# One pass of 32 chunks over both directions of a state-space scan

## The chip, the cores and the metric

The kernel runs on one core of a Trainium2 chip (trn2). The metric is the time of one execution on the device in microseconds, the median of several runs.

## What is computed

A block of three parts over 4 sequences of 2048 tokens with 256 channels: a feed-forward half (attention with 16 heads, then a mixture of 8 experts), a bidirectional state-space layer, and the feed-forward half again. The change touches the state-space layer alone, whose reference, cut to what matters, is:

```python
def _mamba_branch(xz, conv_w, conv_b, x_proj_w, dt_w, dt_b, A_log, D):
    x, z = jnp.split(xz, 2, axis=1)
    x = _silu(causal depthwise conv of 4 taps(x, conv_w) + conv_b)
    dt, Bm, Cm = split(einsum('bdl,ed->bel', x, x_proj_w))      # 16 + 16 + 16 rows
    dt = softplus(einsum('brl,dr->bdl', dt, dt_w) + dt_b)
    A = -jnp.exp(A_log)
    def step(h, inp):
        dt_t, B_t, C_t, u_t = inp
        h = jnp.exp(dt_t[..., None] * A) * h + (dt_t * u_t)[..., None] * B_t[:, None, :]
        return (h, jnp.einsum('bdn,bn->bd', h, C_t))
    ...
    y = ys + D[None, :, None] * x
    return y * _silu(z)
h = _layernorm(x, norm_w, norm_b)
xz = jnp.einsum('bld,ed->bel', h, in_proj_w)
y_f = _mamba_branch(xz, ...the forward weights)
y_r = _mamba_branch(xz[..., ::-1], ...the reverse weights)[..., ::-1]
out = jnp.einsum('bdl,od->blo', y_f + y_r, out_proj_w)
return x + out
```

There are 512 inner channels (4 groups of 128, m = 0 to 3) and 16 states (n = 0 to 15).

## The kernel before

The program is a row of phases. Each phase has its own tiles and semaphores and ends in a barrier of all engines. `mamba_in` writes the inputs of the scans to DRAM (`xp`, padded by three columns, and `zs`, the silu of z). Then `mamba_scan` is called twice, as phase `scan_f` with the forward weights, which writes `y`, and as phase `scan_r` with the reverse weights, which reads `y` and `zs` and writes `yz`, the sum of both directions times silu(z). `mamba_out` multiplies by the output weights.

One call works through N = 16 chunks of 512 tokens, four to a sequence. The five engines each run their own list of the same chunks; nothing but semaphores ties them together, and each engine issues in the order of its list. `in_steps` (L1511) makes that list: the four chunks of the first sequence are written out one after another, the other twelve run in a hardware loop (`Fori`) of three passes with four chunks in the body. In the reverse direction `place` (L1507) counts the chunks from the end.

A chunk is 16 steps, one a state. In step n:

- ACT makes the decays, exp(dt A), into two PSUM banks in turn (L1831), four a step.
- DVE multiplies dt u with the row of b for the next state (`times_b`, L1889; POOL does it for the states in `POOL_N`) and runs the scan along the tokens (L1923), four a step, into one of four buffers `h`. The direction is in the order in which the columns are read (`flip`).
- POOL multiplies h with the row of c (L1628). The rows come from SP, which loads them broadcast (`row_c`, `row_b`) from a small DRAM tensor.
- PE adds h up over the states in PSUM banks 0 to 3 (`sum_state`, L1707), against an identity.

Between these, every engine prepares the chunks to come: PE does the convolution of chunk i + 2 (`conv`, L1647, in halves in steps 7 to 14, through one bank that ACT empties in `conv_out`, L1753, in steps 9, 11, 13 and 15), the projection of chunk i + 1 (`x_proj`, L1664, step 0; `dt_proj`, L1674, steps 3 to 6) and the row of b (`row_b`, L1682). ACT adds the silu (L1757) and the softplus. The window of x for chunk i + 2 is loaded at step 0, the preparation of a chunk past the last one wraps round to chunk 0 and is thrown away.

In step 1 `skip` (L1697) opens the sums with D u, after y of the chunk before has been read. In the reverse direction it also adds the other direction's y (`yi`, L1701). The finished sum is read by ACT in the forward direction (`read_y`, L1797) and by DVE in the reverse one, times silu(z) (L1896), and SP stores it in step 3 (L1536). In the reverse direction SP loads zs into the store's buffer `yo` (L1577) and the next y into `yi` (L1579) in step 5.

Ahead of the first chunk stands a preparation of its own: the weights are loaded (L1550 to L1554), DVE builds the diagonal matrices for the convolution (L1866) and for D (L1870) and negates exp(A_log) (L1873), and chunks 0 and 1 are convolved, chunk 0 also projected, before the first scan.

## Time and profile before

| | us |
|---|---|
| median of 3 runs | 8743.57 |
| lowest and highest of them | 8741.03, 8743.65 |
| the profiled execution | 8750.53 |
| its span in the trace | 8748.8 |
| first scan of the forward direction | 2702.82 |
| first scan of the reverse direction | 4469.96 |
| last result of the reverse direction sent off | 6201.55 |

The profile is of one execution. The chip's engines are PE (TensorE), DVE (VectorE), ACT (ScalarE), POOL (GpSimd) and SP (SyncE, which issues loads and stores here). A row names the line of the kernel, the engine, the operation, output <- inputs and shapes.
### The profile page before, as it was taken

What the parts mean: (1) busy time and instruction counts of PE and PEld (TensorE: products, weight loads), DVE (VectorE), ACT (ScalarE), POOL (GpSimd) and SP (SyncE); (2) the same over time, 40 slices, a digit from 0 to 9 for tenths busy, and PEclk for the clock granted to TensorE, in tenths of its full rate; (3) what the DMA queues carried; (4) which work ended last, traced back from release to release, by engine and by line L of the source; (5) the groups of instructions that cost most, each with busy time, mean ns of one, the idle gap of its engine ahead of it and who ended that gap; (6) DMA issues with size and microseconds to landing.
All of it is one profiled execution on the core that took longest, in us unless ns stands there. A gap on an engine that the chain in (4) does not pass through costs nothing. (4 is left out here: it accounts for less than half of the span.)

```text
span 8748.8 us, 137191 instructions
## 1 busy us (share of the span) xinstructions
PE 7384.9 (84%) x39098; PEld 2876.4 (33%) x39098; DVE 7557.3 (86%) x11017; ACT 5055.9 (58%) x7663; POOL 3676.0 (42%) x1812
## 2 busy tenths in 40 slices
PE   6788888889997888888878888888777888888799
PEld 3222222225543333333323333333542222222255
DVE  6898888878867999999979999999358988888888
ACT  3577777762235666666655555555224777777622
POOL 0010011100006999999969999999300100110000
PEclk8799999999999999999999999999987999999999
DMA  6001001012262222222223333333561011011122
GB/s 171 17 19 20 19 19 26 19 42 77 72 210 88 83 83 82 82 83 84 83 92 100 102 103 100 100 102 100 171 189 17 19 20 19 19 21 23 42 67 67
DMA packets 554170, 623.35 MB, mean 71 GB/s; under 512 B 205376, under 2 KB 363328, under 8 KB 549408
## 3 DMA queue, kind: packets, MB, share of 16 engines
q1 hardware_dynamic: 548896, 581.63, 22.8%
q0 software_dynamic: 4608, 33.56, 1.9%
q8 instruction: 330, 5.41, 0.3%
q14 instruction: 336, 2.75, 0.1%
HBM read 416.65 MB, written 163.76 MB: 66 GB/s over the span
## 5 line engine op out<-in xcount | busy, mean ns | idle before, releaser
L833 DVE TENSOR_REDUCE ffn_att_mx<-psum 128x1 f32<-128x512 f32 (+2 forms) x4840 | 2915.6, 655 | 389.7 <-PE psum L666 197.4
L794 ACT ACTIVATE ffn_att_e<-psum,unscale 128x1024 f32<-128x1024 f32 (+3 forms) x2560 | 2384.0, 983 | 843.9 <-PE psum L739 842.9
L632 POOL TENSOR_SCALAR_AFFINE_SELECT ffn_att_e<-ffn_att_e 128x512 f32<-128x512 f32 x512 | 324.6, 634 | 3125.8 <-ACT ffn_att_e L794 3125.8
L666 PE MATMUL psum<-ffn_att_k,ffn_att_q 48*128 48x512 f16 (+3 forms) x5384 | 989.1, 368 | 611.2 <-DVE ffn_att_mx L833 545.2
L1628 POOL TENSOR_TENSOR scan_r_h<-scan_r_h,scan_r_cs 128x1024 f32<-128x1024 f32 x512 | 1207.1, 2447 | 148.0 <-ACT scan_r_state L1791 144.7
L705 PE MATMUL psum<-ffn_att_e,ffn_att_v 128*32 128x512 f32 (+3 forms) x10240 | 1248.5, 558 | 10.0 <-issue 3.8
L1628 POOL TENSOR_TENSOR scan_f_h<-scan_f_h,scan_f_cs 128x1024 f32<-128x1024 f32 x512 | 1204.4, 2444 | 118.8 <-ACT scan_f_state L1791 116.1
L1707 PE MATMUL psum<-scan_f_h,ident 128*128 128x512 f32 x2048 | 989.0, 623 | 84.0 <-POOL scan_f_h L1628 83.1
L1707 PE MATMUL psum<-scan_r_h,ident 128*128 128x512 f32 x2048 | 975.0, 617 | 78.1 <-POOL scan_r_h L1628 77.5
L1831 ACT ACTIVATE psum<-scan_r_dt,scan_r_an 128x512 f32<-128x512 f32 x1024 | 698.1, 682 | 456.2 <-DVE scan_r_h L1923 456.0
L1831 ACT ACTIVATE psum<-scan_f_dt,scan_f_an 128x512 f32<-128x512 f32 x1024 | 697.6, 681 | 423.8 <-DVE scan_f_h L1923 423.3
L666 PEld LDWEIGHTS psum<-ffn_att_k,ffn_att_q 48*128 48x128 f16 x5384 | 263.9, 94 | 2002.3 <-DVE ffn_att_mx L833 1884.7
L1923 DVE TENSOR_TENSOR_SCAN scan_r_h<-psum,scan_r_state,scan_r_db 128x512 f32<-128x512 f32 x704 | 844.5, 1261 | 5.5 <-ACT psum L1831 5.5
L1923 DVE TENSOR_TENSOR_SCAN scan_f_h<-psum,scan_f_state,scan_f_db 128x512 f32<-128x512 f32 x704 | 840.5, 1261 | 9.0 <-ACT psum L1831 9.0
L739 PE MATMUL psum<-ffn_att_q,ffn_att_k 50*128 50x512 f16 (+3 forms) x5120 | 728.1, 355 | 32.9 <-issue 29.5
L1707 PEld LDWEIGHTS psum<-scan_f_h,ident 128*128 128x128 f32 x2048 | 384.7, 197 | 670.2 <-issue 434.1
L1707 PEld LDWEIGHTS psum<-scan_r_h,ident 128*128 128x128 f32 x2048 | 383.9, 195 | 648.8 <-issue 439.2
L1180 DVE SCALAR_TENSOR_TENSOR ffn_out_acc<-psum,ffn_out_comb,ffn_out_acc 128x256 f32<-128x256 f32 x896 | 433.4, 484 | 65.2 <-PE psum L1045 29.6
L1889 DVE TENSOR_TENSOR scan_r_db<-scan_r_du,psum 128x2048 f32<-128x2048 f32 x177 | 404.9, 2288 | 25.1 <-PE psum L1682 4.8
L1889 DVE TENSOR_TENSOR scan_f_db<-scan_f_du,psum 128x2048 f32<-128x2048 f32 x177 | 404.9, 2288 | 24.7 <-DVE scan_f_h L1923 3.9
L1923 DVE TENSOR_TENSOR_SCAN scan_f_h<-psum,scan_f_state,scan_f_dbp 128x512 f32<-128x512 f32 x320 | 385.9, 1264 | 30.8 <-ACT psum L1831 30.8
L1923 DVE TENSOR_TENSOR_SCAN scan_r_h<-psum,scan_r_state,scan_r_dbp 128x512 f32<-128x512 f32 x320 | 385.9, 1264 | 30.8 <-ACT psum L1831 30.8
(240 smaller groups left out, 9216.5 us busy)
## 6 DMA issues: line engine op xcount, KB each, us to landing
scan_f_cs<-scan_f_bcd SPq DMA_DIRECT2D x264, 256.0 KB, 3.2
scan_r_cs<-scan_r_bcd SPq DMA_DIRECT2D x264, 256.0 KB, 3.3
scan_f_bs<-scan_f_bcd SPq DMA_DIRECT2D x82, 256.0 KB, 3.5
scan_r_bs<-scan_r_bcd SPq DMA_DIRECT2D x82, 256.0 KB, 3.5
scan_f_win<-xp SPq DMA_DIRECT2D x18, 1036.0 KB, 6.6
scan_r_win<-xp SPq DMA_DIRECT2D x18, 1036.0 KB, 7.0
ffn_att_q<-q_parts SPq DMA_DIRECT2D x144, 128.0 KB, 2.9
mamba_out_ys<-yz SPq DMA_DIRECT2D x18, 1024.0 KB, 7.3
```

The source lines that it names most:

```text
L632: nc.gpsimd.affine_select(out=part, in_=part, compare_op=ALU.is_ge, fill=0.0, base=0, pattern=[[0, REP], [1, P]], channel_multiplier=-1).t ...
L666: ins = nc.tensor.matmul(psum[:, turns[hh], j * w:(j + 1) * w], q[at, i // HALF, pair, i % HALF * P:(i % HALF + 1) * P], k[at, c * P:c * P ...
L705: ins = nc.tensor.matmul(psum[32 * h:32 * h + VW, BANK_O, off:CH], V[par][:, kb, :], E[:, s % PB, h, off:CH], start=kb == 0, stop=closes(s ...
L739: ins = nc.tensor.matmul(psum[:, h, off:CH], k[at, kb * P:(kb + 1) * P], q[at, qb * CH // (HALF * P), h // 2, qb * CH % (HALF * P) + off:q ...
L794: nc.scalar.activation(E[:, s % PB, 2 * hp:2 * hp + 2, off:CH], psum[:, 2 * hp:2 * hp + 2, off:CH], ACT.Exp, scale=unscale[:, 0:1]).then_i ...
L833: nc.vector.reduce_max(mx[:, hh * 2 + pairs[0]:hh * 2 + pairs[1], i // HALF, i % HALF, c // TT], psum[:, turn, 0:(pairs[1] - pairs[0]) * w ...
L1180: nc.vector.scalar_tensor_tensor(acc[:, e % 2, :], psum[:, BANKS_E[(n // 2) % 4], (e % 2) * C:(e % 2 + 1) * C], comb[par][:, t, e:e + 1], ...
L1628: nc.gpsimd.tensor_tensor(hh, hh, cs[:, n % NCS, :].unsqueeze(1).to_broadcast([P, 2, CH]), ALU.mult).then_inc(hc_ready, 1)
L1707: ins = nc.tensor.matmul(psum[:, m, :], ident[:, :], h[n % NH][:, m, :], start=False, stop=n == DS - 1)
L1831: nc.scalar.activation(psum[:, BANK_A + k % 2, :], dt[par][:, m, :], ACT.Exp, scale=an[:, m, n:n + 1]).then_inc(decay, 1)
L1889: nc.vector.tensor_tensor(db[b_turn(par, n)][:, :, :], du[par][:, :, :], psum[:, BANK_B, :].unsqueeze(1).to_broadcast([P, DM, CH]), ALU.mu ...
L1923: nc.vector.tensor_tensor_scan(h[n % NH][:, m, flip], psum[:, BANK_A + k % 2, flip], made_b[:, m, flip], state[:, n, m:m + 1], ALU.mult, A ...
```

## The change

The two calls become one, `mamba_scans`, a single phase over M = 32 chunks: 0 to 15 forward, 16 to 31 reverse. Each step gets a function `way(k)`, which says whether the chunk k ahead of the current one is a reverse one; every use of weights, window offset, read order and position asks it. So in forward chunks 14 and 15 the preparation of chunks 16 and 17 uses the reverse weights. The list of chunks is now: four written out, a loop of two passes (4 to 11), eight written out (12 to 19), a loop of three passes (20 to 31).

Both directions' weights, diagonals and negated A are made ahead of chunk 0, those of the reverse direction behind the others'. The addition of the other direction's y becomes a part of its own, `add_other`, in step 9 instead of step 1, and the load of the next `yi` moves from step 5 to step 11. The first `yi` and `zs` are loaded in step 5 of chunk 16.

```diff
-def mamba_scan(nc, tag, psum, ident, reverse, xp, zs, y_other, y_out, conv_w, conv_b, xprojT, dtT, dt_b, a_log, d_w, B, S):
+def mamba_scans(nc, tag, psum, ident, xp, zs, y, yz, weights, B, S):
     N = B * NC
+    M = 2 * N
-    LAST = 0 if reverse else CH - 1
-    flip = slice(None, None, -1) if reverse else slice(None)
+    LAST = (CH - 1, 0)
+    FLIP = (slice(None), slice(None, None, -1))
-    PE_X, PE_DT, PE_CONV = 0, 3, 7
+    PE_X, PE_DT, PE_CONV, PE_Y, SP_Y = 0, 3, 7, 9, 11
...
         def in_steps(eng, step):
-            for r in range(NC):
-                step(r, r % 2, r == 0, r == 0, r == NC - 1)
-            if B > 1:
-                with eng.Fori(0, B - 1) as b:
-                    for r in range(NC):
-                        step(b * NC + NC + r, r % 2, False, r == 0, r == NC - 1)
+            def alone(i):
+                step(i, i % 2, i == 0, i % NC == 0, i % NC == NC - 1, lambda k: i + k >= N)
+
+            def batches(first, count, rev):
+                if count > 0:
+                    with eng.Fori(0, count) as b:
+                        for r in range(NC):
+                            step(b * NC + first + r, r % 2, False, r == 0, r == NC - 1, lambda k: rev)
+            for i in range(NC):
+                alone(i)
+            batches(NC, B - 2, False)
+            for i in range(max(N - NC, NC), N + NC):
+                alone(i)
+            batches(N + NC, B - 1, True)
...
-                if reverse:
-                    sp.dma_start(yi[:, :, :], cols(y_other, place(0))).then_inc(y_in, 16)
+                sp.dma_start(cw[1][:, :, :], weights[1][0]).then_inc(w_in[1], 16)
...
-                        if n == 5 and reverse:
-                            if not first:
-                                hold(sp, stored, 16 * i, sp_passed)
-                            sp.dma_start(yo[:, :, :], cols(zs, place(i))).then_inc(z_in, 16)
-                            hold(sp, y_added, DM * (i + 1), sp_passed)
-                            sp.dma_start(yi[:, :, :], cols(y_other, place(i + 1))).then_inc(y_in, 16)
+                        if n == 5 and way(0):
+                            hold(sp, stored, 16 * i, sp_passed)
+                            sp.dma_start(yo[:, :, :], cols(zs, place(i, True))).then_inc(z_in, 16)
+                            if not way(-1):
+                                sp.dma_start(yi[:, :, :], cols(y, place(i, True))).then_inc(y_in, 16)
+                        if n == SP_Y and way(0):
+                            hold(sp, y_added, DM * (i - N + 1), sp_passed)
+                            sp.dma_start(yi[:, :, :], cols(y, place(i + 1, True))).then_inc(y_in, 16)
...
-                    if reverse:
-                        pe.wait_ge(y_in, 16 * (i + 1))
-                        for m in range(DM):
-                            nc.tensor.matmul(psum[:, m, :], ident[:, :], yi[:, m, :], start=False, stop=False).then_inc(y_added, 1)
+                def add_other(i):
+                    pe.wait_ge(y_in, 16 * (i - N + 1))
+                    for m in range(DM):
+                        nc.tensor.matmul(psum[:, m, :], ident[:, :], yi[:, m, :], start=False, stop=False).then_inc(y_added, 1)
...
                         if n == 1:
-                            skip(i, par, first)
+                            skip(i, par, first, way(0))
+                        if n == PE_Y and way(0):
+                            add_other(i)
...
                 first_silu(1, FREE)
-                act.wait_ge(a_neg, 1)
+                act.wait_ge(w_in[1], 112)
+                nc.scalar.activation(an[1][:, :, :], an[1][:, :, :], ACT.Exp).then_inc(a_exp, 1)
+                act.wait_ge(a_neg, 2)
...
-                        if not reverse and n == 1 and not first:
+                        if n == 1 and not first and not way(-1):
                             read_y(i - 1, m)
...
+                dve.wait_ge(w_in[1], 112)
+                diagonals(1)
+                skips(1)
                 dve.wait_ge(cleared, 2)
...
                 times_b(0, 0, 0)
+                negate(1)
...
-                        if reverse and n == 1 and not first:
+                        if n == 1 and not first and way(-1):
                             read_y(i - 1, m)
```

On ACT, at the change of direction. Before, between the last decay of the forward scan (`scan_f_an`) and the first of the reverse one (L1831 with `scan_r_an`), stand a loop's end, the last reads of y, and the second phase's preparation:

```order
L1831 ACTIVATE psum<-scan_f_dt,scan_f_an 128x512
L1518 REGISTER_ALU
L1518 COMPARE_AND_BRANCH
L1791 ACTIVATE scan_f_state<-scan_f_zeros 128x2
L1797 ACTIVATE scan_f_yo<-psum 128x512 x4
L1526 UNCONDITIONAL_BRANCH
L1745 UNCONDITIONAL_BRANCH
L1747 ACT_TABLE_LOAD
L1749 ACTIVATE scan_r_an<-scan_r_al 128x64
L1801 ACT_TABLE_LOAD
L1801 ACTIVATE scan_r_u<-psum,scan_r_cb 128x512 x4
L1802 ACT_TABLE_LOAD
```

Now, at the same place (`scan_anf` is the forward A, `scan_anr` and `scan_cbr` the reverse A and convolution bias):

```order
L1771 ACTIVATE scan_u<-psum,scan_cbr 128x512
L1775 ACT_TABLE_LOAD
L1775 ACTIVATE scan_u<-scan_u 128x2048
L1776 ACT_TABLE_LOAD
L1851 ACTIVATE psum<-scan_dt,scan_anf 128x512
L1809 ACTIVATE scan_state<-scan_zeros 128x2
L1851 ACTIVATE psum<-scan_dt,scan_anf 128x512
L1851 ACTIVATE psum<-scan_dt,scan_anr 128x512
L1809 ACTIVATE scan_state<-scan_zeros 128x2
L1851 ACTIVATE psum<-scan_dt,scan_anr 128x512 x2
```

The first reverse decay directly follows the last forward one; the reads of y have gone into step 1 of the next chunk.

On DVE, ahead of the first chunk of all. Before:

```order
L1866 TENSOR_SCALAR scan_f_cwd<-ident,scan_f_cw 128x128 x16
L1870 TENSOR_SCALAR scan_f_dwd<-ident,scan_f_dw 128x128 x4
L1873 TENSOR_SCALAR scan_f_an<-scan_f_an 128x64
L1879 TENSOR_TENSOR psum<-psum,scan_f_bc 32x512
L1883 TENSOR_TENSOR scan_f_bc<-psum,scan_f_mid 32x512
L1900 TENSOR_TENSOR scan_f_dt<-scan_f_sp,scan_f_dt 128x2048
L1902 TENSOR_TENSOR scan_f_du<-scan_f_dt,scan_f_u 128x2048
L1889 TENSOR_TENSOR scan_f_db<-scan_f_du,psum 128x2048 x2
L1923 SCALAR_TENSOR_TENSOR scan_f_h<-psum,scan_f_state,scan_f_db 128x512 x4
```

Now (the last letter of `cwd`, `dwd` and `an` is the direction):

```order
L1888 TENSOR_SCALAR scan_dwdf<-ident,scan_dwf 128x128 x4
L1893 TENSOR_SCALAR scan_anf<-scan_anf 128x64
L1883 TENSOR_SCALAR scan_cwdr<-ident,scan_cwr 128x128 x16
L1888 TENSOR_SCALAR scan_dwdr<-ident,scan_dwr 128x128 x4
L1907 TENSOR_TENSOR psum<-psum,scan_bc 32x512
L1911 TENSOR_TENSOR scan_bc<-psum,scan_mid 32x512
L1928 TENSOR_TENSOR scan_dt<-scan_sp,scan_dt 128x2048
L1930 TENSOR_TENSOR scan_du<-scan_dt,scan_u 128x2048
L1917 TENSOR_TENSOR scan_db<-scan_du,psum 128x2048
L1893 TENSOR_SCALAR scan_anr<-scan_anr 128x64
L1917 TENSOR_TENSOR scan_db<-scan_du,psum 128x2048
L1953 SCALAR_TENSOR_TENSOR scan_h<-psum,scan_state,scan_db 128x512 x4
```

Twenty diagonals have come in ahead of the split of b, and a negation between the two products with b.

On PE, steps 8 to 10 of a reverse chunk. Before:

```order
L1647 MATMUL psum<-scan_r_win,scan_r_cwd 128x512 x2
L1707 MATMUL psum<-scan_r_h,ident 128x512 x4
L1682 MATMUL psum<-scan_r_bc,scan_r_sel 128x512
L1647 MATMUL psum<-scan_r_win,scan_r_cwd 128x512 x2
L1707 MATMUL psum<-scan_r_h,ident 128x512 x4
L1682 MATMUL psum<-scan_r_bc,scan_r_sel 128x512
L1647 MATMUL psum<-scan_r_win,scan_r_cwd 128x512 x2
```

Now:

```order
L1657 MATMUL psum<-scan_win,scan_cwdr 128x512 x2
L1719 MATMUL psum<-scan_h,ident 128x512 x4
L1692 MATMUL psum<-scan_bc,scan_sel 128x512
L1657 MATMUL psum<-scan_win,scan_cwdr 128x512 x2
L1713 MATMUL psum<-scan_yi,ident 128x512 x4
L1719 MATMUL psum<-scan_h,ident 128x512 x4
L1692 MATMUL psum<-scan_bc,scan_sel 128x512
L1657 MATMUL psum<-scan_win,scan_cwdr 128x512 x2
```

The four matmuls on `yi`, which stood in step 1 behind those on `dwd`, stand between the half convolution and the sums of step 9.

## Rows read from the trace of the kernel before

**Rows 1.** The page's first part: busy us (share of the span) x instructions.

```profile
PE 7384.9 (84%) x39098; PEld 2876.4 (33%) x39098; DVE 7557.3 (86%) x11017; ACT 5055.9 (58%) x7663; POOL 3676.0 (42%) x1812
```

**Rows 2.** Stretches between first scans: us from:to, length, busy us.

```profile
core 0: us, PE busy (x) PEld busy (x) DVE busy (x) ACT busy (x) POOL busy (x), PEclk, DMA share, GB/s
2702.82:2807.68 104.86, 87.72 (x187) 33.70 (x186) 102.07 (x78) 64.73 (x124) 99.21 (x38) 0.95 0.21 63
2807.68:2912.53 104.85, 89.47 (x197) 33.86 (x195) 102.06 (x79) 66.07 (x127) 102.11 (x40) 0.98 0.28 84
3227.97:3333.62 105.65, 92.21 (x195) 35.03 (x195) 102.06 (x78) 66.06 (x127) 101.97 (x41) 0.95 0.29 83
3439.28:3546.54 107.26, 91.68 (x196) 35.27 (x195) 102.05 (x78) 66.03 (x127) 103.28 (x41) 0.95 0.28 83
3972.22:4291.70 319.48, 269.25 (x585) 102.24 (x585) 306.40 (x232) 198.07 (x381) 304.60 (x118) 0.98 0.28 82
4291.70:4469.96 178.26, 136.92 (x286) 52.69 (x286) 120.40 (x108) 91.54 (x165) 110.31 (x44) 0.90 0.31 95
...
5438.63:5546.67 108.04, 92.33 (x203) 35.52 (x203) 104.45 (x83) 64.39 (x123) 102.21 (x41) 0.98 0.33 101
```

**Rows 3.** Order of time at the change of direction, DVE: start, us, engine.

```profile
4392.90 2.46 DVE L1923 TENSOR_TENSOR_SCAN scan_f_h<-psum,scan_f_state,scan_f_dbp 128x512 f32<-128x512 f32 x2 [1.89 <-ACT psum L1831]
...
4408.42 0.91 DVE L1860 MEMSET scan_r_sel<- 96x1024 uint32 x1 [13.05 <-PEq L51]
...
4469.96 4.81 DVE L1923 TENSOR_TENSOR_SCAN scan_r_h<-psum,scan_r_state,scan_r_db 128x512 f32<-128x512 f32 x4 [0.29 <-ACT psum L1831]
```

**Rows 4.** Order of time at the start of the forward phase.

```profile
2643.69 8.28 DVE L1866 TENSOR_SCALAR scan_f_cwd<-ident,scan_f_cw 128x128 f32<-128x128 f32 x16 [0.30 <-DMA scan_f_cw<-in_m_conv_w_f]
...
2649.17 0.26 ACT L1749 ACTIVATE scan_f_an<-scan_f_al 128x64 f32<-128x64 f32 x1 [5.77 <-DMA scan_f_wt<-in_m_dtT_f]
...
2652.68 0.19 DVE L1873 TENSOR_SCALAR scan_f_an<-scan_f_an 128x64 f32<-128x64 f32 x1
...
2674.51 0.69 DVE L1879 TENSOR_TENSOR psum<-psum,scan_f_bc 32x512 f32<-32x512 f32 x1 [21.64 <-ACT scan_f_bc L1764]
...
2700.24 2.29 DVE L1889 TENSOR_TENSOR scan_f_db<-scan_f_du,psum 128x2048 f32<-128x2048 f32 x1 [3.30 <-PE psum L1682]
2700.73 1.28 ACT L1802 ACT_TABLE_LOAD   x1
```

**Rows 5.** Order of time without a loop's turn, at one, at the exit.

```profile
3439.74 3.63 PE L1664 MATMUL psum<-scan_f_u,scan_f_wx 128*48 128x512 f32 x8
...
3544.34 2.29 DVE L1889 TENSOR_TENSOR scan_f_db<-scan_f_du,psum 128x2048 f32<-128x2048 f32 x1 [1.39 <-issue]
...
3547.68 5.26 PE L1664 MATMUL psum<-scan_f_u,scan_f_wx 128*48 128x512 f32 x8
...
6193.69 7.03 PE L1707 MATMUL psum<-scan_r_h,ident 128*128 128x512 f32 x16
```

**Rows 6.** Order of time, a reverse chunk: PE, then one of ACT.

```profile
5453.96 3.60 PE L1701 MATMUL psum<-scan_r_yi,ident 128*128 128x512 f32 x8
...
5506.81 0.39 PE L1682 MATMUL psum<-scan_r_bc,scan_r_sel 96*128 96x512 bf16 x1 [1.59 <-DVE scan_r_db L1889]
5507.04 1.88 PE L1647 MATMUL psum<-scan_r_win,scan_r_cwd 128*128 128x512 f32 x4
...
5513.01 1.98 PE L1647 MATMUL psum<-scan_r_win,scan_r_cwd 128*128 128x512 f32 x4 [0.66 <-ACT scan_r_u L1753]
...
5525.77 0.39 PE L1682 MATMUL psum<-scan_r_bc,scan_r_sel 96*128 96x512 bf16 x1 [1.31 <-DVE scan_r_db L1889]
...
5512.29 0.67 ACT L1753 ACTIVATE scan_r_u<-psum,scan_r_cb 128x512 f32<-128x512 f32 x1
```

**Rows 7.** The loads into yi: issues, and time to landing.

```profile
L1579 SPq DMA_DIRECT2D scan_r_yi<-y x16: 388/394/1965, 4507.7 to 6128.5; - x16
...
DMA to landing us min/median/max: 6.3/9.5/10.9
```

195 lines of the change are left out of this document (101 added, 94 removed).

## The prediction

> **What bounds the kernel now.** I read the page first, for the busy shares [rows 1]: VectorE (DVE) is busy 86% of the span and TensorE (PE) 84%, but that mean covers attention, projection and scan stages with different limits, so it prices nothing here. The change touches the two scans alone, so the second view is a table of stretches cut at the first DVE scan instruction of a chunk [rows 2]. A chunk (512 tokens, 16 states) of the forward scan takes 104.86 us where its code stands straight in the program and 105.65 us in the hardware loop; DVE is busy 102.07 and 102.06 us of that, PE 87.72 and 92.21, ACT 64.73 and 66.06. DVE is the bound, with 2.8 and 3.6 us of idle per chunk. POOL is nearly as busy (99 to 102 us of a chunk), but it works on states that DVE has already scanned. The reverse chunk takes 108.04 us, since DVE also reads y out there (104.45 us busy), and its idle is 3.6 us again.
>
> Third, the order of time at the change of direction [rows 3]. The last forward scan pair starts at 4392.90 and takes 2.46, so DVE's stream ends at 4395.36. DVE then does nothing for 13.05 us (rest of PE and POOL work, the store of y, the barrier of the phase) until the memset of the reverse phase at 4408.42, and its first scan runs at 4469.96. 74.60 us pass between two scans that in the middle of a direction follow each other directly. In that stretch no engine is a bound for long: it is a chain through all of them, load, diagonals, convolution, silu, projection, softplus, b.
>
> **The change part by part.**
>
> *The boundary.* What the reverse phase computes in those 74.60 us for its first chunk is what every chunk computes for the next one. The forward scan's last chunk already does it today: its steps load, convolve and project a chunk that nobody scans (the position wraps round). So preparing reverse chunk 0 there adds no instruction to the last forward chunk; it only makes the work useful, with other weights. The stretch from the first scan of forward chunk 15 to the first scan of the reverse direction, now 178.26 us [rows 2], becomes one ordinary chunk. The nearest row is a chunk of straight code, since chunks 12 to 19 are written out now: 104.86. Gain 178.26 - 104.86 = 73.40. The reads of y of the last forward chunk stay on ACT and lie in step 1 of the next chunk, as in the other forward chunks, where they cost DVE nothing (104.86 for chunk 0, which has none of them, and 104.85 for chunk 1, which has). The new loads of that chunk: zs into yo and y into yi are issued in step 5, 37.7 us after the first scan (4507.7 for a chunk that starts at 4469.96 [rows 7]), and y into yi lands at most 10.9 us later, at 48.6; PE wants it in step 9, about 63 us after the first scan (for a chunk that starts at 5438.63: PE's row at 5506.81 less its idle of 1.59 and the sums of one state, 3.6 as for four matmuls, is 5501.6 [rows 6]). The store of y that they follow is issued in step 3. 14 us of cover; 0.
>
> *Forward chunks 12 to 15 leave the loop.* Chunks 12 to 14 take 319.48 us together [rows 2]; three straight ones take 3 x 104.86 = 314.58. Gain 4.90. Part of it is a loop turn's echo: after a turn PE comes late, its projection takes 5.26 us against 3.63 [rows 5], the last sums of y stand behind it, and ACT's read of them holds up the next decay.
>
> *One turn of the forward loop becomes an exit.* A chunk that ends in a turn takes 107.26 us against 105.65 [rows 2], and in it DVE shows 1.39 us of "issue" before the first instruction of the next pass [rows 5]. Chunk 11 now ends in a branch not taken. The only exit that the trace shows on a busy engine is PE's out of the reverse loop: 16 records without a gap across it, from 6193.69 for 7.03 us [rows 5]. I take 0 for it, so a gain of 107.26 - 105.65 = 1.61; the bound from the other side is the turn itself and its echo in chunk 12, which is what chunks 12 to 14 take over three loop chunks, 319.48 - 3 x 105.65 = 2.53: so up to 4.1 us less gain. A page of the Trainium skill bears on this (Runtime: NRT & Kernel Launch, Instruction fetch mechanics): fetch ahead is sequential and hidden, and a taken branch whose target is not held costs a fetch. By it the exit and the extra straight code are free, as I have them; were an exit priced as a turn, the gain would be those 4.1 us smaller. The trace agrees on the turn (1.39 us) and on straight code (104.86 against 105.65).
>
> *The set-up of two directions at the start.* Added: seven weight loads on SP, 16 + 4 diagonals and one negation on DVE, one Exp on ACT. SP: the loads stand behind the first direction's, and SP has nothing to do until the second window load, which waits for the first convolutions. DVE: the weights of today had landed by 2649.17, 5.5 us after the first of them [rows 4]; as much again for the seven more is 2654.7. Sixteen diagonals take 8.28 us [rows 4], twenty 10.4, so they end by 2665.1, and DVE's next work is at 2674.51, after 21.64 us of idle. Cover 9.4 us: 0, and if it were gone, 10.4. PE starts on diagonals of the first direction alone and is not held. Not covered is the tail: ACT's Exp of the reverse A comes after the table load that ends at 2702.01 (2700.73 + 1.28), takes 0.26, and DVE must negate the result (0.19 us) ahead of its second product with b, because the negation stands ahead of it in DVE's order. That product started at 2700.24; it now starts at 2702.01 + 0.26 + 0.19 and a tenth for a semaphore, some 2702.5, and its 2.29 us put the first scan at about 2704.8 instead of 2702.82. PE and SP shift with it. Cost 2.0.
>
> *The other direction's y is added in step 9, not step 1.* PE only: four matmuls, 3.60 us [rows 6], in 16 reverse chunks. At step 1 they cost DVE nothing today (the chunk's idle is 3.6 in both directions), so nothing is gained there. At step 9 they fall between half a convolution and the sums. PE then lags 3.60 us, less the 1.59 us that it waited for DVE before the next row of b at 5506.81: 2.0. The half convolution behind it would end at 5508.92 + 2.0 = 5510.9, and ACT fetches its result at 5512.29 [rows 6]: 1.4 us of cover. With the idle of 0.66 and 1.31 us that follow, PE is level again at 5526. DVE needs the sums of state 8 at state 12 (four h buffers), some 10 us later. 0, at most 3.6 a chunk. SP's load of the next yi moves to step 11, behind a wait for that addition; behind this wait stand rows of c fetched eight states ahead, and the yi itself is wanted a chunk later. 0.
>
> Sum: -73.40 - 4.90 - 1.61 + 2.0 = -77.9 us. The profiled execution took 8750.5 (span 8748.8) and should become 8672.6 (span 8670.9); it lies 7 us above the median of the runs, 8743.57, from which I take the same 77.9: **8665.7 us**.
>
> **The rivals.**
>
> 1. *The exit costs like a turn*, with its echo: 4.1 us less, 8669.8. For it: nobody has seen DVE or ACT leave a loop busy. Against: PE's exit.
> 2. *The second set-up is not hidden*: the small loads come late or the diagonals are in front of something: +10.4, 8676. For it: many small loads behind a 1 MB window. Against: 9.4 us of cover. The Trainium skill (DMA: Bandwidth & Descriptors, Specifications) has transfers under 512 B below line rate; by it the seven loads (conv_b's rows are 16 B) would land later than their bytes suggest, which the first seven's 5.5 us already contain.
> 3. *The boundary is only half closed*: the first reverse chunk waits at some hand-over that the forward chunks don't have (zs or y into the buffers, stored before read). With half of 73.4 lost, 8702. Against: 14 us of cover.
> 4. *The addition in step 9 comes through once a chunk*: 16 x 3.6 = 58 us given back, 8723, at the edge of what can be told from no change. Against: 1.4 us of cover at ACT, and 2.0 of lag in all, so it needs a worse lag than the rows show, for instance a PE as slow just there as in the projection at 3547.68.
> 5. *It comes through three times a chunk, and the kernel is slower.* PE never makes up the lag, and each of ACT's three fetches of a convolution in steps 11, 13 and 15 waits the full 3.6 us; ACT issues in order, so the decays and with them DVE wait. 16 x 10.8 = 173 us, 8839. The change is a loss from 78/16 = 4.9 us a chunk on. For it: PE is busy 92 us of 108. Against: 15.7 us of PE idle a chunk, 3.6 of them in the three gaps of [rows 6].
>
> **How the numbers follow.** Forecast 0.68; exit 0.10; set-up 0.09; half closed 0.04; once a chunk 0.06; three times 0.03. The range takes the forecast and rivals 1 and 2 (0.87 together). Its low end is the forecast less what the remaining forward turn may cost less (1.6, and a late chunk behind it, 2.5) and 4 us for the scatter of runs; its high end is rival 2 with the same: 8658 to 8680. About 0.2%, 17.5 us, is what a measurement can tell from no change. Faster by more: forecast, rivals 1 to 3 and half of 4, 0.94; within: the other half of 4, 0.03; slower: 0.03.
>
> **What would show it.** In the trace after: the first scan near 2704.8, and no idle of DVE over 3 us between two scans until the end of the reverse direction; 104.9 us from the first scan of chunk 15 to the first of chunk 16; chunks 12 to 14 at 104.9 each; reverse chunks in the loop at 108.0 as before; no memsets and no phase barrier between the directions. Wrong if reverse chunks are longer than 108.0 with ACT's convolution fetch showing idle behind PE, or if chunk 16 shows PE waiting for yi.

## The result, and the profile after

The changed kernel takes 8701.18 us (median of 5 runs, 8692.50 to 8705.29) against 8743.65 (5 runs beside it, 8741.03 to 8765.72): ratio 0.9942, interval 0.9928 to 0.9957. It is faster by 42 us; the forecast had 78. The profiled execution took 8692.50, its span is 8690.8.

The page's first part, as [rows 1] of before:

```profile
span 8690.8 us, 135894 instructions
...
PE 7349.9 (85%) x39016; PEld 2870.6 (33%) x39016; DVE 7538.8 (87%) x11009; ACT 5034.7 (58%) x7630; POOL 3672.6 (42%) x1809
```

DVE's busy time fell by 18.5 us and PE's by 35.0; the span fell by 58.0. So idle time went too. The two traced executions lie apart by more than the medians do (58.0 against 42.5 us): the one of before is 7 us above its median, the one of after the fastest of its five. Where did the time go? The first thing to do is to cut both traces at the first work of each phase:

| from / to | before | after | difference |
|---|---|---|---|
| start / first work of the scan phase | 2642.11 | 2641.77 | -0.3 |
| scan phase / first of `mamba_out` | 3565.21 | 3489.34 | -75.9 |
| `mamba_out` | 171.85 | 171.62 | -0.2 |
| second feed-forward, preparation | 153.02 | 153.32 | +0.3 |
| second attention (`ffn_att`) | 1746.78 | 1726.89 | -19.9 |
| second `ffn_out` to the end | 469.85 | 507.86 | +38.0 |
| sum | | | -58.0 |

The scan phase gave what was forecast for it, within 2 us. Two later phases, whose code nobody touched, differ by twenty and by forty microseconds with opposite signs.

*The scans.* Stretches between first scans, after, in the columns of [rows 2]: chunk 11 (now an exit), chunks 12 to 14, chunk 15, a reverse chunk in the loop, and one whose predecessor ended in a turn; last the second `ffn_out`:

```profile
core 0: us, PE busy (x) PEld busy (x) DVE busy (x) ACT busy (x) POOL busy (x), PEclk, DMA share, GB/s
...
3865.20:3970.75 105.55, 90.98 (x195) 34.63 (x195) 102.05 (x78) 66.05 (x127) 101.89 (x41) 0.97 0.28 83
3970.75:4286.51 315.76, 274.04 (x585) 105.65 (x585) 306.18 (x232) 198.00 (x381) 305.65 (x118) 0.95 0.28 83
4286.51:4391.35 104.84, 90.62 (x196) 34.49 (x195) 102.05 (x78) 66.03 (x127) 101.97 (x40) 0.97 0.28 84
5361.30:5469.33 108.03, 93.90 (x204) 36.40 (x203) 104.44 (x82) 64.41 (x123) 102.20 (x41) 0.97 0.32 101
5251.46:5361.30 109.84, 95.71 (x203) 36.93 (x203) 104.56 (x83) 64.36 (x123) 100.96 (x40) 0.94 0.33 99
8182.94:8687.10 504.16, 462.31 (x2304) 262.45 (x2304) 382.41 (x964) 128.87 (x256) 35.30 (x18) 0.95 0.23 71
```

Chunk 15, which was 178.26 us to the first reverse scan, is an ordinary chunk: 104.84. Order of time there, the last forward scan and the first reverse one (compare [rows 3]):

```profile
4386.65 2.46 DVE L1953 TENSOR_TENSOR_SCAN scan_h<-psum,scan_state,scan_dbp 128x512 f32<-128x512 f32 x2 [2.05 <-ACT psum L1851]
...
4387.97 0.69 ACT L1851 ACTIVATE psum<-scan_dt,scan_anr 128x512 f32<-128x512 f32 x1 [0.65 <-DVE scan_h L1953]
...
4389.15 2.29 DVE L1917 TENSOR_TENSOR scan_db<-scan_du,psum 128x2048 f32<-128x2048 f32 x1
...
4391.35 4.80 DVE L1953 TENSOR_TENSOR_SCAN scan_h<-psum,scan_state,scan_db 128x512 f32<-128x512 f32 x4
```

DVE idles 2.05 us before the last forward pair (1.89 before), and from there its instructions follow each other; ACT makes the first reverse decay (`scan_anr`) during that pair. The 13.05 us of the hand-over and everything to 4469.96 are gone.

The start of the phase, DVE and ACT (compare [rows 4]):

```profile
2674.06 0.69 DVE L1907 TENSOR_TENSOR psum<-psum,scan_bc 32x512 f32<-32x512 f32 x1 [17.62 <-ACT scan_bc L1782]
...
2700.23 1.28 ACT L1820 ACT_TABLE_LOAD   x1
2701.53 0.26 ACT L1834 ACTIVATE scan_anr<-scan_anr 128x64 f32<-128x64 f32 x1
2701.81 0.20 DVE L1893 TENSOR_SCALAR scan_anr<-scan_anr 128x64 f32<-128x64 f32 x1 [5.33 <-ACT scan_anr L1834]
2701.92 2.28 DVE L1917 TENSOR_TENSOR scan_db<-scan_du,psum 128x2048 f32<-128x2048 f32 x1
...
2704.12 3.63 DVE L1953 TENSOR_TENSOR_SCAN scan_h<-psum,scan_state,scan_db 128x512 f32<-128x512 f32 x3
```

The twenty extra diagonals are hidden: DVE is still idle for 17.62 us before the split of b at 2674.06. The tail is seen as priced: table load, Exp (`scan_anr`), negation, product, one after the other, the first scan at 2704.12. That is 62.35 us after the phase's first work against 60.71.

Step 9 of the same reverse chunk as in [rows 6] (PE, then ACT's fetch of the convolution):

```profile
5424.71 3.60 PE L1713 MATMUL psum<-scan_yi,ident 128*128 128x512 f32 x8
...
5428.15 3.60 PE L1719 MATMUL psum<-scan_h,ident 128*128 128x512 f32 x8
...
5431.58 0.38 PE L1692 MATMUL psum<-scan_bc,scan_sel 96*128 96x512 bf16 x1
...
5431.80 1.88 PE L1657 MATMUL psum<-scan_win,scan_cwdr 128*128 128x512 f32 x4
...
5434.96 0.67 ACT L1771 ACTIVATE scan_u<-psum,scan_cbr 128x512 f32<-128x512 f32 x1
```

The addition of `yi` stands between half a convolution and the sums; the half convolution behind it ends at 5433.68, ACT fetches it at 5434.96. 1.3 us of cover are left and DVE's chunk is 108.03.

*The second `ffn_out`.* DVE's waits in it, and the order of time around one of them on DVE and on PE:

```profile
engine line waited for: us in total, times, longest us
DVE ffn_out_acc L1180 <- issue: 42.3, 6, 7.5
...
8271.03 0.19 DVE L1168 TENSOR_TENSOR ffn_out_comb<-ffn_out_lg,ffn_out_rden 128x32 f32<-128x32 f32 x1 [0.23 <-DVE ffn_out_lg L1165]
8278.47 0.48 DVE L1180 SCALAR_TENSOR_TENSOR ffn_out_acc<-psum,ffn_out_comb,ffn_out_h 128x256 f32<-128x256 f32 x1 [7.25 <-issue]
...
8279.54 0.61 PE L1045 MATMUL psum<-ffn_out_eh,ffn_out_uh 128*128 128x512 f16 x1 [3.96 <-DVE ffn_out_acc L1180]
```

Before the first of the accumulations of an expert (L1180) DVE stands still for 7.25 us though it waits for no semaphore; its inputs are there, and PE's next matmul (L1045) waits 3.96 us for DVE. The place is the turn of the loop: the trace's record of DVE's own branches has the branch back to the loop's start at 8271.13 and the next instruction at 8278.16. This happens six times, at each of the six turns of the seven passes, 61 us apart (8278.5, 8339.7, 8400.8, 8463.0, 8524.2, 8585.7), 42.3 us in all. Before, the same stretch had none of it, nor has the first `ffn_out` of the changed kernel (466.44 us), which runs the same code. Both `ffn_out` of before, DVE busy as long as after:

```profile
1916.64:2383.16 466.52, 450.00 (x2304) 260.78 (x2304) 382.69 (x964) 128.88 (x256) 35.23 (x18) 0.98 0.24 76
8278.97:8745.20 466.23, 450.02 (x2304) 260.80 (x2304) 382.67 (x964) 128.86 (x256) 35.25 (x18) 0.97 0.24 76
```

The trace also shows what arrives in such a wait. The page's list of DMA queues has two of the kind `instruction`; this is one of them before, after, and in the first experiment below:

```profile
q14 instruction: 336, 2.75, 0.1%
...
q14 instruction: 359, 2.94, 0.1%
...
q14 instruction: 330, 2.70, 0.1%
```

In the changed kernel it moves 8192 bytes five times after each of the six turns of the second `ffn_out`: after the first turn at 3.09, 5.01, 7.64, 10.43 and 38.65 us from the branch, with DVE going on at 7.03. In the kernel before there is not one transfer of that kind between the first and the last turn of either `ffn_out`.

*The second attention.* The stretch of before, then that of after:

```profile
6532.19:8276.41 1744.22, 1415.73 (x12821) 415.39 (x12821) 1515.10 (x2626) 1228.58 (x1378) 163.32 (x258) 0.93 0.11 20
```

```profile
6456.05:8180.37 1724.32, 1397.29 (x12821) 411.12 (x12821) 1512.68 (x2626) 1229.57 (x1378) 164.06 (x258) 0.94 0.12 20
```

19.9 us shorter with as many instructions; DVE is busy 2.4 us less, PE 18.4 us less, ACT 1.0 us more. PE's busy time points at its clock: the trace's record of the granted clock has 237.5 us of this stretch at the lower of the two levels (1.2 GHz) before and 190.3 us after.

### The profile page after: what moved, and what is told of

Its sections match the earlier page's. It is cut to its first block and busy times, and to the rows that moved or that the text cites. A ratio compares the mean times of both kernels' runs of the same rounds, so it can differ in the third digit from the quotient of the medians.

```text
span 8690.8 us, 135894 instructions
## 1 busy us (share of the span) xinstructions
PE 7349.9 (85%) x39016; PEld 2870.6 (33%) x39016; DVE 7538.8 (87%) x11009; ACT 5034.7 (58%) x7630; POOL 3672.6 (42%) x1809
## 5 line engine op out<-in xcount | busy, mean ns | idle before, releaser
L1638 POOL TENSOR_TENSOR scan_h<-scan_h,scan_cs 128x1024 f32<-128x1024 f32 x1024 | 2412.6, 2449 | 206.0 <-ACT scan_state L1809 200.6
L1719 PE MATMUL psum<-scan_h,ident 128*128 128x512 f32 x4096 | 1985.8, 626 | 158.1 <-POOL scan_h L1638 156.9
L1953 DVE TENSOR_TENSOR_SCAN scan_h<-psum,scan_state,scan_db 128x512 f32<-128x512 f32 x1408 | 1684.6, 1260 | 10.5 <-ACT psum L1851 10.5
L1719 PEld LDWEIGHTS psum<-scan_h,ident 128*128 128x128 f32 x4096 | 781.8, 199 | 1325.1 <-issue 906.0
L1851 ACT ACTIVATE psum<-scan_dt,scan_anr 128x512 f32<-128x512 f32 x1024 | 698.0, 682 | 456.1 <-DVE scan_h L1953 455.6
L1851 ACT ACTIVATE psum<-scan_dt,scan_anf 128x512 f32<-128x512 f32 x1024 | 697.5, 681 | 421.4 <-DVE scan_h L1953 420.9
L1917 DVE TENSOR_TENSOR scan_db<-scan_du,psum 128x2048 f32<-128x2048 f32 x353 | 807.4, 2287 | 37.5 <-issue 4.2
L1953 DVE TENSOR_TENSOR_SCAN scan_h<-psum,scan_state,scan_dbp 128x512 f32<-128x512 f32 x640 | 771.7, 1264 | 62.3 <-ACT psum L1851 62.3
L1629 POOL TENSOR_TENSOR scan_dbp<-scan_du,scan_bs 128x2048 f32<-128x2048 f32 x160 | 731.1, 4570 | 0.0
L1180 DVE SCALAR_TENSOR_TENSOR ffn_out_acc<-psum,ffn_out_comb,ffn_out_acc 128x256 f32<-128x256 f32 x896 | 433.3, 484 | 62.8 <-PE psum L1045 26.9
L1045 PE MATMUL psum<-ffn_out_eh,ffn_out_uh 128*128 128x512 f16 x1024 | 393.8, 385 | 25.2 <-DVE ffn_out_acc L1180 25.2
L1045 PE MATMUL psum<-ffn_out_el,ffn_out_uh 128*128 128x512 f16 x1024 | 393.4, 384 | 0.0
L1045 PE MATMUL psum<-ffn_out_eh,ffn_out_ul 128*128 128x512 f16 x1024 | 393.0, 384 | 0.0
```

Of the source, the lines that this page charges most:

```text
L1045: ins = nc.tensor.matmul(psum[:, BANKS_E[n % 4], :], u[:, k, t * P:(t + 1) * P], w[:, k, 2 * e:2 * e + 2, :], start=k == 0 and p == 0, sto ...
L1629: nc.gpsimd.tensor_tensor(dbp[:, :, :], du[par][:, :, :], bs[turn][:, :].unsqueeze(1).to_broadcast([P, DM, CH]), ALU.mult).then_inc(pool_b, 1)
L1638: nc.gpsimd.tensor_tensor(hh, hh, cs[:, n % NCS, :].unsqueeze(1).to_broadcast([P, 2, CH]), ALU.mult).then_inc(hc_ready, 1)
L1719: ins = nc.tensor.matmul(psum[:, m, :], ident[:, :], h[n % NH][:, m, :], start=False, stop=n == DS - 1)
L1851: nc.scalar.activation(psum[:, BANK_A + k % 2, :], dt[par][:, m, :], ACT.Exp, scale=an[way(0)][:, m, n:n + 1]).then_inc(decay, 1)
L1917: nc.vector.tensor_tensor(db[b_turn(par, n)][:, :, :], du[par][:, :, :], psum[:, BANK_B, :].unsqueeze(1).to_broadcast([P, DM, CH]), ALU.mu ...
```

## The experiments

Theory F (fetch): the six waits of 7 us are the time to fetch DVE's instructions. The transfers of kind `instruction` above speak for it; what decides whether they come is open. The loop of `ffn_out` is 275 instructions of DVE's list long; by F what counts is only where in the program it starts, and the added straight code of the scans moved it by 485 instructions. The Trainium skill (Runtime: NRT & Kernel Launch, Instruction fetch mechanics) describes such a store: refilled in blocks of 256 instructions, two of them held (more for PE), and "A taken branch whose target isn't in the current 2-page window forces a DMA fetch of the target page". By it a loop of 275 instructions that lies across two blocks runs from what is held, and one that lies across three fetches in each pass; a start modulo 256 decides, and, as an estimate from the page's block and the 275 instructions, 18 starts of 256 are bad. Rival T: the stall comes from the single phase or from timing (what POOL, ACT or the queues are left with). Rival L: any longer list is bad, wherever it starts.

A pad below is a row of cheap instructions that compute nothing, at the end of an engine's list of the scans.

**20 instructions more in the changed kernel.**

```diff
                 for m in range(DM):
                     read_y(M - 1, m)
+                for k in range(20):
+                    nc.vector.memset(pad[:, k:k + 1], 0.0)
```

> The changed kernel with 20 small DVE memsets of a tile that nothing reads, at the end of the scan phase, behind the last read of y. They change nothing but where DVE's code of the later phases lies: the loop of ffn2_out (L932) starts 505 instead of 485 instructions further on than in the kernel before. Theory placement (the 42.3 us of 'issue' that DVE shows before L1180 in ffn2_out, once in each of six passes and 7.1 us long, is a fetch of code that depends on where the loop lies): it is gone, ffn2_out takes 466 us as in ffn1 and before, and the kernel some 41 us less than the changed one, 8652 for its profiled 8692.5, with 1.5 us for the memsets already in it. The Trainium skill (Runtime: NRT & Kernel Launch, Instruction fetch mechanics) has blocks of 256 instructions of which two are held; by it, as an estimate, 20 instructions push the start of this loop of 275 instructions past a block's edge, so that it lies in two blocks instead of three. Rival, chance (the stall belongs to a state of the chip or to the shorter scans, whatever the placement): six waits of 7 us again, 8690. Rival, read of the page but wrong edge: the stall stays or moves to another line, at the same price.

8659.49 us (4 runs; ratio to the kernel before 0.9895, interval 0.9879 to 0.9912). The waits are gone; DVE's longest waits in the second `ffn_out`, and that stretch:

```profile
DVE ffn_out_acc L1180 <- PE psum L1045: 14.9, 49, 0.6
DVE ffn_out_lg L1144 <- PE psum L1032: 14.5, 16, 5.5
...
8178.74:8645.51 466.77, 450.03 (x2304) 261.00 (x2304) 382.67 (x964) 128.88 (x256) 35.24 (x18) 0.97 0.24 76
```

The transfers between the turns are gone too. 20 instructions that do nothing make the changed kernel 42 us faster by the medians (8701.18 and 8659.49), 37 of them in this stretch. Rival L falls.

**229 instructions more in the kernel before.** 485 modulo 256 is 229. The scans are those of before; only the start of DVE's code behind them moves.

```diff
                 if reverse:
                     for m in range(DM):
                         read_y(N - 1, m)
+                    for k in range(229):
+                        nc.vector.memset(pad[:, k:k + 1], 0.0)
```

> The kernel before with 229 small DVE memsets behind the last read of y of the reverse scan, nothing else. 229 is what the change's shift of 485 DVE instructions leaves over a whole block of 256 (that figure is the page's, named below). Theory placement: DVE waits some 7 us in each of six passes of ffn2_out, at L1180, 42 us in all, though nothing of the change is there; the memsets themselves cost 229 x 0.06 = 14 us or less, part of it under the store of y; so 8743.6 + 42 + 8 to 14 = 8794 to 8800. Rival, chance: ffn2_out takes 466 us, and the kernel 8752 to 8758. The figure of 256 instructions to a block is that of the Trainium skill (Runtime: NRT & Kernel Launch, Instruction fetch mechanics); if blocks have another size, this kernel would show no stall and the first of this set still could.

8784.08 us (6 runs; ratio 1.0037, interval 1.0025 to 1.0050). DVE's first wait in the second `ffn_out`, and that stretch:

```profile
DVE ffn_out_acc L1180 <- issue: 44.4, 6, 7.8
...
8275.07:8779.98 504.91, 463.56 (x2304) 262.55 (x2304) 382.28 (x964) 128.87 (x256) 35.27 (x18) 0.95 0.23 71
```

The stall is there without any part of the change, with the same five transfers a turn. Rival T falls with it. The kernel is 10 to 16 us faster than was expected: the scans with the memsets are 1.2 us longer in the traces, not 8 to 14, and the second attention took 1733.1 us in place of 1744.2.

**256 and 9 instructions more in the changed kernel.** As the first experiment, with 256 and with 9 memsets. 256 leaves the start modulo 256 as it is in the changed kernel; 9 shifts it a little.

> The changed kernel with 256 small DVE memsets at the end of the scan phase instead of 20. Theory placement with a period of 256 instructions (the figure of the Trainium skill, Runtime: NRT & Kernel Launch, Instruction fetch mechanics): the loop of ffn2_out lies as in the changed kernel without memsets, so the six waits of about 7 us are back, ffn2_out takes 504 us, and the kernel about 8700 plus some 8 to 14 for the memsets. Rival, any shift by memsets away from the changed kernel's place cures it (a longer period, or a bad spot of a few instructions alone): ffn2_out 466 us, 8668 to 8674.

8695.24 us (2 runs, ratio 0.9938, 0.9918 to 0.9958); the second `ffn_out` takes 504.06 us with six waits of 6.65 to 7.27: one whole block further, the same stall. (The 8708 to 8714 expected had 8 to 14 us for the memsets; the scan phase is 3.7 us longer than in the changed kernel.)

> The changed kernel with 9 small DVE memsets at the end of the scan phase: ffn2_out's loop starts 494 DVE instructions further on than before. 484 and 485 showed the stall, 505 did not. If the stall needs the 275 instructions of the loop to touch three blocks, it is there for a run of neighbouring starts and ends at one edge between 485 and 505; this run halves the stretch. Stall: about 8700; no stall: about 8659. It tells only where the edge is, both outcomes fit the theory; a wait of another size than 7 us, or at another line, would not.

8702.93 us (2 runs, ratio 0.9946, 0.9927 to 0.9966):

```profile
DVE ffn_out_acc L1180 <- issue: 51.4, 12, 7.5
...
8188.46:8699.92 511.46, 463.67 (x2304) 262.96 (x2304) 382.32 (x964) 128.85 (x256) 35.27 (x18) 0.95 0.23 70
```

Twelve waits now: six of 6.6 to 7.45 us and six of 1.55 to 1.80 at the next L1180, 7 us more in all. By what was written down before this run, a wait of another size would not fit F. The short waits stand before the sixth instruction of the loop, just when the third transfer after the branch arrives (7.86 us after the branch, the wait from 8.04 to 9.77). So they can be read as a block's edge five instructions behind the loop's start. Read so, and with 18 bad starts, the bad shifts would be 225 to 242, an estimate that every start below agrees with; the reading itself was not tested by another run. With the starts of all kernels (shift of DVE's code against the kernel before, modulo 256):

| shift | kernels | waits of 7 us |
|---|---|---|
| 0 | before, and before with the step-9 addition or with pads on PE and ACT | none |
| 2 | all chunks straight (shift 1282) | none |
| 105 | the first `ffn_out`, in every kernel | none |
| 228 | before with chunks 12 to 15 unrolled (484) | six |
| 229 | changed (485), before + 229, changed + 256, before + pads on all | six |
| 238 | changed + 9 | six, and six short ones |
| 249 | changed + 20 | none |

The bad starts lie within one run that holds 228 to 238 and ends before 249, as F has it. In every one of the six kernels with waits the `instruction` queue makes 30 transfers of 8192 bytes between the first and the last turn of the second `ffn_out`, five a turn; in the eight others, and in the first `ffn_out` of all fourteen, none. So the waits are waits for code, and its place decides.

**One part alone: forward chunks 12 to 15 out of the loop, in the kernel before.**

```diff
-            if B > 1:
-                with eng.Fori(0, B - 1) as b:
-                    for r in range(NC):
-                        step(b * NC + NC + r, r % 2, False, r == 0, r == NC - 1)
+            passes = B - 1 if reverse else B - 2
+            with eng.Fori(0, passes) as b:
+                for r in range(NC):
+                    step(b * NC + NC + r, r % 2, False, r == 0, r == NC - 1)
+            if not reverse:
+                for r in range(N - NC, N):
+                    step(r, r % 2, False, r % NC == 0, r % NC == NC - 1)
```

> The kernel before with forward chunks 12 to 15 written out behind a loop of two passes, as the changed kernel has them; two phases, the set-ups and the addition in step 1 stay. Theory, my terms of the sum: chunks 12 to 15 take 104.86 us each and chunk 11 loses the loop's turn, so the forward scan is 4.9 + 0.8 + 1.6 = 7.3 us shorter; if the exit costs like a turn, 3.2. Theory placement: DVE's code of ffn2_out now starts 484 instructions further on than before, one less than in the changed kernel, so the stall of 42 us comes with it and the kernel is slower than before by 35 us, 8779, though its scans are faster. Rival, chance: ffn2_out at 466 us and 8736.

8764.10 us (10 runs; ratio 1.0021, 1.0012 to 1.0031). Chunk 11 takes 105.90 us, chunks 12 to 14 314.97 (forecast of 314.58), chunk 15 to the first reverse scan 177.38 instead of 178.26: 6.5 us gained in the scans, as priced. And the kernel is slower, because of this:

```profile
DVE ffn_out_acc L1180 <- issue: 44.7, 6, 7.7
...
8253.93:8758.18 504.25, 460.74 (x2304) 261.76 (x2304) 382.25 (x964) 128.89 (x256) 35.28 (x18) 0.96 0.22 71
```

44.7 us of waits, lost four thousand microseconds later against 6.5 gained: a part of the change that is right by its own sum is a loss. It is a smaller one than the 8779 expected, since the second attention took 1723.0 us here.

**One part alone: the addition in step 9, in the kernel before.**

```diff
-    PE_X, PE_DT, PE_CONV = 0, 3, 7
+    PE_X, PE_DT, PE_CONV, PE_Y, SP_Y = 0, 3, 7, 9, 11
...
                         if n == 1:
                             skip(i, par, first)
+                        if n == PE_Y and reverse:
+                            add_other(i)
```

> The kernel before with the addition of the other direction's y in step 9 and the load of the next yi in step 11 of the reverse scan, nothing else; DVE's code is the same. My prediction's term: 0, reverse chunks at 108.0 us in the loop, 8743.6. Rival 4: up to 3.6 us a chunk, 58 in all. In the changed kernel the reverse chunks show 108.04, so the former; what this run adds is whether the addition in step 1 had cost anything: then it would be faster by up to 16 x 0.4.

8749.48 us (10 runs; ratio 1.0003, 0.9994 to 1.0013), reverse chunks 108.03 to 108.05. It costs nothing: the forecast's 0, and rivals 4 and 5 are out.

**The tail of the set-up.** The changed kernel with the 20 memsets; ACT's Exp and DVE's negation of the reverse A stand earlier, where both engines wait.

```diff
                 middle(0, 0)
+                act.wait_ge(w_in[1], 112)
+                nc.scalar.activation(an[1][:, :, :], an[1][:, :, :], ACT.Exp).then_inc(a_exp, 1)
...
                 split_low(0, 0)
+                negate(1)
```

> The changed kernel with 20 memsets as in e1, and the reverse direction's A made earlier: ACT's Exp behind the middle split of chunk 0 (where ACT waits for PE's dt projection), DVE's negation behind the low split, where DVE waits 12 us for the softplus. Prediction's term of 2.0 us, measured as 1.6 in the changed kernel (first scan 62.35 us after the phase's first instruction, 60.71 before): it goes, first scan at 60.7 and the kernel at 8659.5 - 1.6 = 8657.9. Rival: the 1.6 us came from the seven loads or the diagonals and stay.

8659.56 us (4 runs, ratio 0.9896, 0.9880 to 0.9913), the same as without it. In the trace the first scan is 60.80 us after the phase's first work, against 62.35 and, before, 60.71: the 1.6 us are what was said, but too small for the runs to tell.

**All 32 chunks written out.** As the last, with no loop in the scans at all and a pad of one.

```diff
-            for i in range(NC):
-                alone(i)
-            batches(NC, B - 2, False)
-            for i in range(max(N - NC, NC), N + NC):
-                alone(i)
-            batches(N + NC, B - 1, True)
+            for i in range(M):
+                alone(i)
```

> As e7, but all 32 chunks written out, no hardware loop in the scan phase, and one memset in place of 20; DVE's loop of ffn2_out starts 1282 instructions further on than before, which is 5 x 256 + 2, so next to the place that the kernel before has. Theory, straight code is fetched for free: every forward chunk 104.86 us and every reverse one 107.24, against the chunks of e1 a gain of 9.5 us forward and 13.9 in reverse, 23 in all, no stall in ffn2_out: 8657.9 - 23 = 8635. Rival, long straight code has a price of its own (fetch of PE's or ACT's lists): chunks above 105.0 and 107.4. Rival, placement of other loops (attention, projection) moves as DVE's did: ffn2_att above 1745 us or ffn2_in above 150.

8638.08 us (4 runs; ratio 0.9870, 0.9853 to 0.9886), the fastest kernel here, 1.3% below the kernel before. A forward and a reverse chunk:

```profile
4288.24:4393.09 104.85, 90.62 (x196) 34.47 (x195) 102.06 (x78) 66.05 (x127) 101.93 (x40) 0.97 0.28 84
4605.17:4712.41 107.24, 92.14 (x204) 35.70 (x203) 104.44 (x82) 64.41 (x123) 102.12 (x40) 0.98 0.34 101
```

104.85 and 107.24, against 105.65 and 108.03 in the loops; the scan phase takes 3467.3 us (3489.34 in the changed kernel). Not every chunk is so short: three forward ones take 105.06 to 105.34 us, and six of the reverse ones 107.8, with some 0.6 us of waiting for the row of b. By the limits written down before the run (105.0 and 107.4) a small part of the rival is there, some 5 us in all; the forecast was 8635. The second `ffn_out` takes 466.47, without the stall, as its start (shift 2) promised.

**The second attention.** In the changed kernel and the six experiments whose lists are longer on all engines it took 1723.0 to 1726.8 us; in the kernel before, with the addition in step 9 and with 229 memsets on DVE 1744.2, 1739.9 and 1733.1. The first attention, whose code lies the same in all kernels, takes 1728.6 to 1739.8 in all of them, so 11 us of scatter come with the same code and nothing changed ahead of it. Theory P: it is the place of PE's or ACT's code, as the fetch is for DVE. Three kernels, the one before with pads behind the reverse scan: 379 matmuls of one column on PE, 547 copies of one column on ACT, and both; the lists are then as long as in the changed kernel.

```diff
                 sum_state(N - 1, DS - 1)
+                if reverse:
+                    pe.wait_ge(cv_sb, DM * (N + 2))
+                    for k in range(379):
+                        nc.tensor.matmul(psum[:, BANK_X, 0:1], ident[:, :], ident[:, 0:1], start=True, stop=True)
```

> The kernel before with 379 one-column matmuls into the convolution's bank at the end of TensorE's list of the reverse scan, and nothing else moved: TensorE's code of the second attention then starts where it does in the changed kernel. The time of the second attention alone (ffn2_att) is looked at; the pad itself lies ahead of it and costs some tens of us. If TensorE's shifted code makes the second attention shorter: 1723 to 1727 us, as in the changed kernel and in six of the experiments. If not: 1733 to 1744 us, as in the kernel before. VectorE's list isn't moved, so the first loop of ffn2_out has no 7 us waits (about 466 us) under every theory.

> The kernel before with 547 one-column copies at the end of ScalarE's list of the reverse scan, which puts ScalarE's code of the second attention where it is in the changed kernel; TensorE's and VectorE's lists are not moved. If ScalarE's shifted code shortens the second attention: 1723 to 1727 us. If not: 1733 to 1744 us. ffn2_out about 466 us.

> The kernel before with both pads, 379 one-column matmuls and 547 one-column copies. If the placement of the two lists is the cause, together or one alone: the second attention takes 1723 to 1727 us. If it is neither, 1733 to 1744 us, and the cause is in VectorE's list (483 instructions longer in the changed kernel) or in something that no list's length shows. ffn2_out about 466 us.

One run each: the second attention took 1738.0, 1736.8 and 1732.5 us, the first two in the band of "not these" and the third half a microsecond below it. The pads themselves cost their own time ahead of it (8910, 8783 and 8907 us in all). None of the three reaches the 1723 to 1727 us of placement; with one run each and 11 us of scatter that speaks against PE's and ACT's lists and is no proof.

**All five lists as long as in the changed kernel.** The last kernel adds 485 memsets on DVE, 232 on POOL and 175 instructions of waits already met on SP to the two pads.

> The kernel before with a pad of cheap instructions at the end of every engine's list of the reverse scan: 379 one-column matmuls (TensorE), 485 one-column memsets (VectorE), 547 one-column copies (ScalarE), 232 one-column memsets (GpSimd), 175 instructions of waits already met (SyncE). All five lists are then exactly as long, to an instruction, as in the changed kernel, while the scans are those of the kernel before. ffn2_out: the fetch theory (only the start of VectorE's code counts) expects what the changed kernel has, about 504 us with six waits of 6.6 to 7.5 us; a theory by which the stall comes from the single phase or the timing of the scans expects 466 us. ffn2_att: if placement of code shortens the second attention, 1723 to 1727 us as in the changed kernel; if placement is not the cause, 1732 to 1744 us as in the kernel before and with two lists padded. The kernel's own time means nothing: the pads cost about 200 us.

One run, 8933.74 us with the pads. The second attention and the second `ffn_out`:

```profile
DVE ffn_out_acc L1180 <- issue: 43.6, 6, 7.5
...
6694.30:8421.62 1727.32, 1399.83 (x12821) 411.90 (x12821) 1514.42 (x2626) 1228.34 (x1378) 163.31 (x258) 0.94 0.11 20
8424.18:8928.36 504.18, 462.19 (x2304) 262.22 (x2304) 382.29 (x964) 128.86 (x256) 35.27 (x18) 0.95 0.22 71
```

The second `ffn_out` takes what it takes in the changed kernel (504.18 and 504.16), with the scans of the kernel before: the strongest test of F. The second attention, 1727.3 us, is 0.3 us outside the band of placement and 5 us below the lowest of the kernels without it. So both phases behave as in the changed kernel once all lists are as long. For the attention this is one run, and which list does it (DVE's alone gave 1733.1) isn't settled.

One rival has no run of its own, but the traces speak to it: TensorE's granted clock. A long and a short first attention, in the kernel with all chunks written out and in the one with 20 memsets:

```profile
185.37:1924.76 1739.39, 1413.00 (x12821) 414.86 (x12821) 1514.26 (x2626) 1229.99 (x1378) 163.42 (x258) 0.93 0.11 20
...
183.94:1912.47 1728.53, 1398.58 (x12821) 411.12 (x12821) 1514.36 (x2626) 1228.99 (x1378) 163.31 (x258) 0.94 0.11 20
```

The same code, and PE's busy time differs by 14.4 us; 226.5 and 191.4 us of the two stretches are granted at 1.2 GHz. Over all 28 attentions of the fourteen traces, first and second, a line through length against time at 1.2 GHz rises by 0.39 us a microsecond (correlation 0.97) and none lies more than 3.4 us off it. By it the 47.2 us less of 1.2 GHz in the changed kernel's second attention are worth 18.5 of its 19.9 us. So the phase gets shorter along with the time at the higher clock. That is a correlation, no run sets the clock; that PE is busy 18.4 us less with the same matmuls fits the clock as the cause. Why more of it was granted remains open. The second attentions of the seven kernels with 1723.0 to 1726.8 us and of the one with all lists padded have 189 to 200 us at 1.2 GHz, the six others 210 to 238, with no overlap, which is hardly chance; but the first attentions, which no edit touches, go from 191 to 227 as well.

## Why the prediction was wrong

By its steps:

- *Boundary, -73.40*: -73.42 measured. *Chunks 12 to 14, -4.90*: 315.76 instead of 319.48, -3.7; chunk 12 (105.58) and 13 (105.33) keep part of an echo and chunk 14 is 104.86. *Turn to exit, -1.61*: chunk 11 is 105.55 instead of 107.31, -1.8, so rival 1 is out. With 1.7 us less at the remaining turn (chunks 7 and 8, 214.35 to 212.69) and 0.6 more in chunk 0 (105.44), 79.9 us are gone from the first forward to the first reverse scan, the sum of the three terms to the tenth, in part by luck.
- *Start-up, +2.0*: +1.64. The cover of the diagonals, put at 9.4 us, is 17.6 (the idle that is left). Rival 2 is out.
- *First `yi` and `zs`, 0*: the load into `yi` was issued 37.7 us after the first reverse scan, as said, and took at most 8.2 us to land; PE added it at 4452.0, 60.7 us after that scan. 0. Rival 3 is out.
- *Step 9, 0*: 0 (108.03 a chunk, and the experiment alone).
- *Reverse chunks as before*: the whole direction takes 1726.51 us from first scan to the end of the last instead of 1723.84, +2.7, at the chunks that follow a turn (109.84 and 109.28). PE stands there 1.3 to 2.4 us "issue" before the row of b and in the projection; I take it for fetching after the turn, but that is argued, not tested. With all chunks straight these waits are gone.

The step that failed is the sentence "By it the exit and the extra straight code are free, as I have them", and with it a sum that ended at the last scan. Straight code is free where it stands; it was not free for what stands behind it. It moved DVE's 275-instruction loop of the second `ffn_out` to a start at which every turn waits for code, 42.3 us in six waits: +38.0 us in the span, half of the forecast gain. The sum had no term for it, and no rival either. The length of the loop and its start in DVE's list could have been counted beforehand, and the 1.39 us of "issue" in [rows 5] showed that a turn has a price of its own. What the trace of before could not give is 7 us a pass, since no loop in it lay badly.

The other miss went the other way and partly hid the first: the second attention is 19.9 us shorter in these two traces, along with 47.2 us less at 1.2 GHz. Without either the profiled execution would show -76, against the -77.9 of the sum. The medians hold less of the attention's share: 42.5 us gained are those 76, less 38.0, and 4 more. With the 20 memsets the kernel is 86.7 us below the kernel before beside it (8659.49 and 8746.17), which is those 76 and 11 more. The median 8659.49 would lie in the range forecast, but the way there goes through two phases that the sum did not hold.

## What to carry to other kernels

When a change makes a program longer or shorter, compare every phase behind it and not only the one that was edited; subtract the phases before judging the edit. A loop whose body on one engine is a little over 256 instructions can run freely or stall about 7 us in each pass, depending on how many instructions stand ahead of it: look for "issue" waits of several microseconds once a pass, and for transfers of the kind `instruction` beside them, and move the start by some cheap instructions ahead of it (here 20 were enough and 9 were not; a body below 256 instructions was not tried). A phase boundary between two similar pipelines is worth what the trace shows between the last step of one and the first of the other, less one ordinary step: here 73.4 us forecast and 73.4 found.
